# Two expert networks reordered: bias products one expert later, routing in pieces, the last expert's first layer early and its activation by blocks

## What is computed

```python
def _L1_ffn_ref(x, Wr, Wi, bi, Wo, bo):      # 8 experts, top 2
    router_logits = jnp.einsum('th,eh->te', xf, Wr)
    topk_vals, topk_idx = jax.lax.top_k(router_logits, TOP_K)
    routing_weights = jax.nn.softmax(topk_vals, axis=-1)
    h = jax.nn.gelu(jnp.einsum('th,efh->etf', xf, Wi) + bi[:, None, :], approximate=False)
    expert_out = jnp.einsum('etf,ehf->eth', h, Wo) + bo[:, None, :]
    ...
def expert_ffn(x, W1, B1, W3, B3, W2, B2):   # L2_ffn, 8 experts and a shared one
    g = swiglu((jnp.einsum('td,edh->teh', x, W1) + B1) * (jnp.einsum('td,edh->teh', x, W3) + B3))
    return jnp.einsum('tei,eid->ted', g, W2) + B2
def swiglu(h):
    xg = jnp.minimum(h[..., ::2], LIMIT)
    xl = jnp.clip(h[..., 1::2], -LIMIT, LIMIT)
    return xg * jax.nn.sigmoid(ALPHA * xg) * (xl + 1.0)
```

## Time and profile before

| | |
|---|---|
| median of 3 runs | 1476.81 us (1475.11, 1476.81, 1479.4) |
| profiled execution, its own time | 1474.77 us |
| its span | 1472.9 us |
| mean granted clock of PE | 0.967 of 2.4 GHz |
| first expert network | about 786 to 903 us of the span |
| second expert network | about 991 to 1307 us |

### The profile page before, as it was taken

How to read it: one execution, slowest core, us unless ns; L and a number is a source line. 1 busy time by engine, 2 the same in 40 slices (tenths; PEclk the granted TensorE clock), 3 DMA queues, 4 the chain that set the end, 5 groups by cost and what they waited for, 6 DMA issues and landing times.

```text
span 1472.9 us, 24074 instructions
## 1 busy us (share of the span) xinstructions
PE 1365.5 (93%) x10014; PEld 1159.6 (79%) x10014; DVE 986.2 (67%) x1782; ACT 773.5 (53%) x1246; POOL 207.3 (14%) x103
## 2 busy tenths in 40 slices
PE   9999999999999798888798999788999999987998
PEld 8999433899433795687697999777999999976976
DVE  8746777646777657566677677676577677757455
ACT  3446888435888354354544454544355544435433
POOL 0110876000876000102001000000000000000100
PEclk9999999999999999999899999899999999988999
DMA  8456353246363131035243453163454555041100
GB/s 346 118 197 210 92 178 86 71 159 211 100 175 91 65 130 54 0 141 208 81 171 130 149 168 125 28 231 129 133 190 167 193 189 193 34 195 74 54 1 22
DMA packets 30834, 194.81 MB, mean 132 GB/s; under 512 B 4211, under 2 KB 4339, under 8 KB 14726
## 3 DMA queue, kind: packets, MB, share of 16 engines
q1 hardware_dynamic: 30726, 193.27, 38.6%
HBM read 183.03 MB, written 3.93 MB: 127 GB/s over the span
## 4 chain that ended last, share of the span: by engine, by line
PE 75%; DVE 13%; ACT 6%; POOL 3%; issue 1%; DMA 0%; DVEq 0%; SPq 0%; ACTq 0%; POOLq 0%
PE PS L357 59%; PE PS L977 6%; PE PS L986 5%; PE PS L362 3%; DVE WL L300 2%; POOL WK L1172 2%; PE PS L618 1%; PE PS L459 1%; POOL WL L307 1%; DVE SM L534 1%; ACT WH L293 1%; DVE SM L1344 1%; ACT WK L1729 1%; DVE WK L1754 1%; DVE WK L1759 1%
## 5 line engine op out<-in xcount | busy, mean ns | idle before, releaser
L300 DVE TENSOR_TENSOR WL<-w,WH 128x768 fp32r<-128x768 f32 x373 | 355.0, 963 | 211.6 <-ACT WH L293 208.9
L293 ACT ACTIVATE WH<-w 128x768 fp32r<-128x768 f32 x381 | 315.9, 841 | 271.9 <-PE PS L357 258.1
L357 PE MATMUL PS<-XS,WH 128*128 128x256 f32 x2292 | 417.9, 285 | 11.4 <-DVE XS L484 7.1
L357 PEld LDWEIGHTS PS<-XS,WH 128*128 128x128 f32 x2292 | 355.8, 190 | 15.6 <-issue 12.0
L357 PE MATMUL PS<-XS,WL 128*128 128x256 f32 x1146 | 324.0, 283 | 0.0
L357 PEld LDWEIGHTS PS<-XS,WL 128*128 128x128 f32 x1146 | 217.6, 190 | 0.0
L1110 DVE TENSOR_TENSOR WK<-PS,WK 128x1024 f32<-128x1024 f32 x128 | 156.7, 1224 | 55.5 <-ACT PS L1054 54.5
L1172 POOL TENSOR_TENSOR WK<-WK 128x1024 f32<-128x1024 f32 x64 | 152.8, 2390 | 206.0 <-ACT WK L1051 206.0
L357 PE MATMUL PS<-WH,GS 128*128 128x256 f32 x864 | 162.0, 286 | 8.0 <-DVE GS L484 6.5
L1054 ACT ACTIVATE PS<-PS 128x1024 f32<-128x1024 f32 x128 | 129.4, 1011 | 34.4 <-PE PS L977 34.4
L357 PEld LDWEIGHTS PS<-WH,GS 128*128 128x128 f32 x864 | 137.1, 192 | 10.6 <-DVE GS L484 7.4
(11 more groups left out here) (252 smaller groups left out, 2014.3 us busy)
## 6 DMA issues: line engine op xcount, KB each, us to landing
w<-f2W_in SPq DMA_DIRECT2D x40, 1152.0 KB, 5.5
w<-Wrel_in SPq DMA_DIRECT2D x12, 1152.0 KB, 7.8
WK<-qrep_in SPq DMA_DIRECT2D x16, 768.0 KB, 5.5
w<-f1Wi_in SPq DMA_DIRECT2D x8, 1152.0 KB, 6.6
w<-f1Wo_in SPq DMA_DIRECT2D x8, 1152.0 KB, 5.1
w<-f3Wqkv_in SPq DMA_DIRECT2D x6, 1152.0 KB, 13.5
RT<-qg_rows SPq DMA_DIRECT2D x16, 384.0 KB, 6.3
RT<-AS SPq DMA_DIRECT2D x32, 192.0 KB, 6.7
```

The lines of the kernel that those rows point to most:

```text
L293: A.e.activation(w_hi(i), w_raw(i), ACT.Copy).then_inc(*hi("w", i))
L300: V.e.tensor_tensor(w_lo(i), w_raw(i), w_hi(i), ALU.subtract).then_inc(*lo("w", i))
L357: ins = T.e.matmul(o, l, r, start=i == 0 and first, stop=i == n - 1 and last, skip_group_check=lint)
```

## The change

All in the two expert networks; no matmul is added or removed.

- First network, PE: up(0), first tile of up(1), logits, rest of up(1), down(0), transpose of the routing weights (`comb_pe`), up(2), bias products, down(1), and on as before. DVE does the routing in three pieces, ahead of the second and third block of expert 1 and behind the third, copies to XN at the head of expert 2, and adds the bias after expert 2's blocks. ACT's Exp stands after expert 1's blocks.
- Second network, first experts: the routing comes in six pieces, one after each block of b(0); PE's order is a(0), logits, b(0), a(1), transpose, down(0), bias products, b(1).
- Second network, every expert up to 7: the clamp of hl now waits for the clamp of hg (`gated`).
- Second network, last expert: PE's order is a(7), down(6), b(7), a(8), b(8), down(7), down(8), with the weights fetched in that order. Its activation is done block by block: clamp of hg after block 2, then for each of blocks 3 to 5 the other three DVE instructions and ACT's upper part; ACT feeds one weight tile ahead of each upper part. The three lower parts follow after block 5.
- `vec_top2` is split into `top2_rank` (one row half) and `top2_pick`, `vec_softmax8` loses its first two instructions to `vec_less8`, with the same instructions in them.

```diff
-if e:
+if 0 < e < 8:
     main.append(("f2c" + str(e - 1), "f2W2", e - 1, 3, "V"))
 main.append(("f2b" + str(e), *(("f2W3", e) if e < 8 else ("f2Ws3", None)), 6, "V"))
+    main.append(("f2c7", "f2W2", 7, 3, "V"))
     main.append(("f2c8", "f2Ws2", None, 3, "V"))
...
-def bias_vec(name, n):
+def comb_vec(name, n):
     V.wait_ge(pe, name + "cT")
     V.e.tensor_copy(XN[0:n, 0:256], ps(name + "cT")[0:n, 0:256]).then_inc(*vec(name + "cT"))
+
+def bias_vec(name, down0):
     for m in range(2):
         for c0, c1 in ((0, 512), (512, 768)):
             V.wait_ge(pe, name + "b", m, c0)
+            V.wait_ge(vec, down0, 0, c0, m)
             V.e.tensor_tensor(x3[:, m, c0:c1], x3[:, m, c0:c1], ps(name + "b", m, c0)[:, 0:c1 - c0],
                               ALU.add).then_inc(*vec(name + "b", m, c0))
...
-    for e in range(8):
-        pe_gemm_T(("f1u", e), f1up(e), 0, 3, xs_at, lambda f: (act, "gelu", e, f),
-                  (lambda k: T.wait_ge(vec, "lower", "f1a", k - k % 2)) if e == 0 else None)
-        if e == 0:
-            logits_pe("f1z", "f1Wr", "f1a")
-        if e == 1:
-            bias_pe("f1", lg, 8, "f1bo")
-        if e:
-            down(e - 1)
+    def up(e, f0, f1, before=None):
+        pe_gemm_T(("f1u", e), f1up(e), f0, f1, xs_at, lambda f: (act, "gelu", e, f), before)
+
+    up(0, 0, 3, lambda k: T.wait_ge(vec, "lower", "f1a", k - k % 2))
+    up(1, 0, 1)
+    logits_pe("f1z", "f1Wr", "f1a")
+    up(1, 1, 3)
+    down(0)
+    comb_pe("f1", lg, 8)
+    up(2, 0, 3)
+    bias_pe("f1", 8, "f1bo")
+    down(1)
+    for e in range(3, 8):
+        up(e, 0, 3)
+        down(e - 1)
     down(7)
...
-        if e == 0:
+        if e == 1:
             act_softmax8("f1", lg)
...
+    def route(part_):
+        if part_ == 0:
+            V.wait_ge(pe, "f1z")
+            V.e.tensor_copy(lg, logits("f1z")).then_inc(*vec("f1zraw"))
+            top2_rank("f1", lg, 8, 0)
+        elif part_ == 1:
+            top2_rank("f1", lg, 8, 1)
+            top2_pick("f1", 8)
+            vec_less8("f1", lg)
+        else:
+            V.wait_ge(act, "f1exp")
+            V.e.tensor_tensor(lg, lg, sm2("f1sel", 8), ALU.mult).then_inc(*vec())
+            vec_norm8("f1", lg)
+            vec.also("f1comb")
+
     for e in range(8):
+        if e == 2:
+            comb_vec("f1", 8)
         for k in range(3):
             feed_vec(ahead(f1up(e) + k))
+            if e == 1 and k:
+                route(k - 1)
             vec_lower(GH[e % 2][:, 1, k, :], gtmp[:, k, :], GH[e % 2][:, 0, k, :], "gelu", e, k)
-        if e == 0:
-            V.wait_ge(pe, "f1z")
-            V.e.tensor_copy(lg, logits("f1z")).then_inc(*vec("f1zraw"))
-            sel = vec_top2("f1", lg, 8)
-            vec_softmax8("f1", lg)
-            V.e.tensor_tensor(lg, lg, sel, ALU.mult).then_inc(*vec())
-            vec_norm8("f1", lg)
-            vec.also("f1comb")
         if e == 1:
-            bias_vec("f1", 8)
+            route(2)
+        if e == 2:
+            bias_vec("f1", "f1d")
         if e:
             down(e - 1)
...
-        else:
+        elif e == 1:
+            comb_pe("f2", comb9, 9)
+            down(0)
+            bias_pe("f2", 9, "f2B2")
+        elif e < 8:
             down(e - 1)
         pe_gemm_T(("f2b", e), f2("b", e), 0, 6, xs_at, lambda f: (vec, "f2h3", e, f))
-        if e == 0:
-            bias_pe("f2", comb9, 9, "f2B2")
+    down(7)
...
+        elif e < 8:
             act_gemm_N(None, f2("c", e - 1), 3, 768)
-        act_gemm(f2("b", e), 6)
+        act_gemm(f2("b", e), 6 if e < 8 else 3)
         A.wait_ge(vec, "f2min", e)
         A.e.activation(sgb[i], hb[i][:, 0:3, :], ACT.Sigmoid, scale=1.702).then_inc(*act("f2sig", e))
-        A.wait_ge(vec, "f2g", e)
         if e >= 2:
             A.wait_ge(pe, ("f2d", e - 2), 512, 1)
-        act_upper(GH[i][:, 0, :, :], hb[i][:, 3:6, :], "f2g", e)
+        if e < 8:
+            A.wait_ge(vec, "f2g", e, 2)
+            act_upper(GH[i][:, 0, :, :], hb[i][:, 3:6, :], "f2g", e, 2)
+    for k in range(3):
+        feed_act(ahead(f2("b", 8) + 3 + k))
+        A.wait_ge(vec, "f2g", 8, k)
+        act_upper(GH[0][:, 0, k, :], hb[0][:, 3 + k, :], "f2g", 8, k)
+    act_gemm_N(None, f2("c", 7), 3, 768)
...
-    def route():
...
+    def route(f):
+        if f == 0:
+            V.wait_ge(act, "f2exp")
+            vec_norm8("f2", sc8)
+            V.e.tensor_tensor(sg, sc8, col("f2gb").unsqueeze(1).broadcast_to((P, 2, 8)), ALU.add).then_inc(*vec())
...
+        elif f == 4:
+            top2_rank("f2top", sg, 8, 0)
+        else:
...
     for e in range(9):
         i = e % 2
+        hg, hl = hb[i][:, 0:3, :], hb[i][:, 3:6, :]
         vec_gemm(f2("a", e), 6)
         if e == 0:
-            route()
-        else:
+            V.wait_ge(pe, "f2z")
+            V.e.tensor_copy(sc8, logits("f2z")).then_inc(*vec("f2zraw"))
+            vec_less8("f2", sc8)
+        elif e == 1:
+            comb_vec("f2", 9)
+            down(0)
+            bias_vec("f2", "f2d")
+        elif e < 8:
             down(e - 1)
 
...
+            if e == 0:
+                route(f)
+            if e == 8 and f == 2:
+                V.wait_ge(vec)
+                V.e.tensor_scalar(hg, hg, 7.0, None, ALU.min).then_inc(*vec("f2min", e))
+            if e == 8 and f >= 3:
+                gated(slice(f - 3, f - 2), f - 3)
+
+        def gated(ks, k):
+            V.wait_ge(vec)
+            V.e.tensor_scalar(hl[:, ks, :], hl[:, ks, :], 7.0, -7.0, ALU.min, ALU.max).then_inc(*vec())
+            V.wait_ge(vec)
+            V.e.scalar_tensor_tensor(out=hl[:, ks, :], in0=hl[:, ks, :], scalar=1.0, in1=hg[:, ks, :],
+                                     op0=ALU.add, op1=ALU.mult).then_inc(*vec())
+            V.wait_ge(vec)
+            V.wait_ge(act, "f2sig", e)
+            V.e.tensor_tensor(hl[:, ks, :], hl[:, ks, :], sgb[i][:, ks, :], ALU.mult).then_inc(*vec("f2g", e, k))
...
         vec_gemm(f2("b", e), 6, second)
-        hg, hl = hb[i][:, 0:3, :], hb[i][:, 3:6, :]
-        V.wait_ge(vec)
-        V.e.tensor_scalar(hg, hg, 7.0, None, ALU.min).then_inc(*vec("f2min", e))
-        V.e.tensor_scalar(hl, hl, 7.0, -7.0, ALU.min, ALU.max).then_inc(*vec())
-        V.wait_ge(vec)
-        V.e.scalar_tensor_tensor(out=hl, in0=hl, scalar=1.0, in1=hg, op0=ALU.add, op1=ALU.mult).then_inc(*vec())
-        V.wait_ge(vec)
-        V.wait_ge(act, "f2sig", e)
-        V.e.tensor_tensor(hl, hl, sgb[i], ALU.mult).then_inc(*vec("f2g", e))
-        vec_lower(GH[i][:, 1, :, :], hl, GH[i][:, 0, :, :], "f2g", e)
-        if e == 0:
-            bias_vec("f2", 9)
+        if e < 8:
+            V.wait_ge(vec)
+            V.e.tensor_scalar(hg, hg, 7.0, None, ALU.min).then_inc(*vec("f2min", e))
+            gated(slice(0, 3), 2)
+            vec_lower(GH[i][:, 1, :, :], hl, GH[i][:, 0, :, :], "f2g", e, 2)
+            for k in range(2):
+                vec.also("lower", "f2g", e, k)
+        else:
+            for k in range(3):
+                vec_lower(GH[0][:, 1, k, :], hl[:, k, :], GH[0][:, 0, k, :], "f2g", 8, k)
+    down(7)
```

More of the change, by code:

```diff
@@ L2188, in vec_top2, with vec_less8 @@
             return sel
-        def vec_softmax8(name, z):
+        def vec_top2(name, val, n):
+            for m in range(2):
+                top2_rank(name, val, n, m)
+            return top2_pick(name, n)
+        def vec_less8(name, z):
             mx = sm(name + "mx", 2)
@@ L2219, in bias_pe @@
             ins.then_inc(*pe(name + "cT"))
+        def bias_pe(name, n, width):
             T.wait_ge(vec, name + "cT")
@@ L2461, in down @@
                 pe_gemm_N(("f2d", e), f2("c", e), 3, 768, gh_at(e % 2), lambda c, m: (vec, "f2d", e, c, m),
-                          lambda k: T.wait_ge(vec, "lower", "f2g", e))
+                          lambda k: T.wait_ge(vec, "lower", "f2g", e, k))
             for e in range(9):
@@ L2483, in first @@
                     if e >= 2:
-                        A.wait_ge(vec, "lower", "f2g", e - 2)
+                        A.wait_ge(vec, "lower", "f2g", e - 2, 2)
                     b1 = col("f2Bs1", f, 1) if e == 8 else col("f2B1", e * 6 + f, 1)
@@ L2519, in down @@
                 vec_gemm_N(("f2d", e), f2("c", e), 3, 768, out_)
-            def route():
-                V.wait_ge(pe, "f2z")
-                V.e.tensor_copy(sc8, logits("f2z")).then_inc(*vec("f2zraw"))
-                vec_softmax8("f2", sc8)
-                vec_norm8("f2", sc8)
-                sg, gs = sm2("f2sg", 8), sm2("f2gs", 4)
-                V.e.tensor_tensor(sg, sc8, col("f2gb").unsqueeze(1).broadcast_to((P, 2, 8)), ALU.add).then_inc(*vec())
-                V.wait_ge(vec)
-                V.e.tensor_reduce(gs, sg.rearrange("p m (g a) -> p m g a", a=2), AX.X, ALU.add).then_inc(*vec())
-                keep = vec_top2("f2grp", gs, 4)
-                V.e.tensor_scalar(keep, keep, 1.0, -BIG, ALU.subtract, ALU.mult).then_inc(*vec())
-                V.wait_ge(vec)
-                for m in range(2):
```

(29 more changed lines are left out.)

38 lines of the change are left out of this document (22 added, 16 removed).

## The result

| | before | after |
| --- | --- | --- |
| median of 6 runs each, us | 1477.02 (1474.68 to 1485.66) | 1458.71 (1456.66 to 1467.35) |
| ratio after/before, 95% interval | | 0.9887 [0.9856, 0.9918] |
| profiled execution, its own time / span | 1474.77 / 1472.9 | 1458.04 / 1456.3 |

The change saves 18.3 us, 1.1%, beyond the 0.3% that counts here. The forecast was 1457.0 for the median and 1455.8 for the profiled execution.

What follows compares the result with a forecast made beforehand. TensorE, busy 93% of the span, bounds the kernel; only its waits and lower-clock time can be won. Gains of 24.3 less 5.3 of new waits net 19.0: 1455.8 profiled, 1457.0 with 1.2 added; range 1451 to 1463.

Steps and rivals of the forecast that it cites:

- First network, 6.4: First network: XN wait gone 3.2, bias products at full clock 1.5, dense matmuls no longer slowed 1.7; 6.4 us saved.
- 2.1 at expert 1: Second network, expert 1's first layer: routing pieces make VectorE's clamp late, so PE loses 2.1 us waiting for weights.
- 7 x 0.12: Second network, seven boundaries from expert 1 on: the added wait between two clamps costs 0.12 us each, 0.8 in all.
- 2.4 at the last expert: Last expert: split activation makes VectorE and ScalarE take turns, 3.8 us a block; waits of 0.75 and 1.65 us.
- The last expert's 7.2: End of second network: PE's 5.58 us wait goes, and 1.6 us of dense matmuls at the lower clock; 7.2 saved.
- Clock at the new waits: PE's waits of 2.1, 0.75 and 1.65 us may or may not bring the clock down; costed at nothing.
- The 1.5 us for the weight tile behind the unbroken routing: Second network's first expert: PE's wait for a weight tile goes, 1.5 us of the 10.7 saved there.
- no new wait: Rival for the whole change: VectorE fills its own gaps and all 24.3 us come; 1451.7 us, 12%.
- twice as long: Rival at the new waits: they are twice as long, 5.3 us more; 1462.3 us, 12%.
- the Exp comes so late: Rival in the first network: PE waits for the combine weights and the 6.4 us stay; 1463.4 us, 5%.
- slower: Rival at the second network's tight boundaries: wider ones keep bringing the clock down, 56 us lost; 1513 us, 2%.
- The clock falls at two of the new waits: Rival at the new waits: two clock falls at 1.7 us each, 3.4 us more; 1460.4 us, 18%.

Runs made afterwards that it cites:

- two-edit kernel: Kernel before with only the bias products one expert later in both networks and the last expert's first layers early; medians 1458.49 and 1457.55 us.
- the kernel with the cut router: Two-edit kernel with the router's 24 narrow passes cut into four between tiles of expert 0's first layer, in both networks; 1460.46 us.

## Why the prediction was right, point by point

The verdict and the place were right, and the sum was 2.2 us too low for the profiled execution (1455.8 against 1458.04). That the median came as close as 1.7 us is in part luck: the same kernel's other two series have 1465.83 and 1460.67, with clock falls in code that the change does not touch, and the first of them lies outside the stated range of 1451 to 1463.

- **First network, 6.4**: 6.24. It holds, and the runs without pieces show that the new place of the bias products alone makes it. No wait for the combine weights appeared.
- **Products at 2.7**: 2.84, from 5.48 at the lower level; they follow the clock.
- **2.1 at expert 1**: 2.19. The minimum starts at 1017.92, 2.7 us behind the layer's end on PE at 1015.2 (1000.78 + 6 x 2.15 + the fall's 1.5), where 2.5 was worked out. That the fall came ahead of it changed little: without it the wait was 2.25 and 2.34.
- **7 x 0.12**: 0.12 in the period; without the added wait 0.7 us of the stage came back.
- **2.4 at the last expert**: 0.84 + 1.40 = 2.24, block period 3.82 for 3.8. The cause is narrower than "DVE and ACT take turns": ACT rounds a weight tile one block too late.
- **The last expert's 7.2**: the 5.58 us wait and its fall are gone; by itself 7.2 in the stage and 7.3 in medians.
- **The 5.3 of new waits in all**: 310.70 against the 305.7 of the two-edit kernel at like clock, 5.0.
- **Clock at the new waits, costed at nothing**: nothing at 0.84 and 1.40 in any of the six profiles that have them. The 2.2 us wait saw a fall in two of seven, both times in the profiles without one behind the router's products. A fall costs 1.5 us, where 1.7 was taken. The Trainium skill, TensorE: Matmul & The Clock Gate, section "A second HAM failure mode: psum-queue depth-cycling", ties falls to short idle gaps between groups of matmuls; that was not borne out at 0.84 and 1.40 us, and at 2.2 us in two profiles of seven.
- **The step that was off** is "Clock at the new waits": it looked for falls only where PE pauses, and left the router's products out. The row it read a pause from, is itself such a group: 24 products of 128x2, near whose end the clock fell. It does so in all fourteen profiles, so pause and narrow products can't be told apart there. The fall behind the second network's router took 1.1 of the 1.9 us by which that network missed (10.7 for 12.6), by the 41.34 and 40.23 us above; the other 0.8 was not traced. The rest is 0.2 in the first network, and, where nothing was edited, 0.7 ahead of it, 0.2 behind the second, less 0.5 in the graph layer; together 2.4 us of span, 2.2 of the executions' own times.
- **The 1.5 us for the weight tile behind the unbroken routing** was no gain of its own: without the pieces the wait nearly goes too, and a clock fall stands in its place (26.52 for 26.29 us).
- **The rivals**: "no new wait" fell, all three chains are serial as said; "twice as long" fell, by 2.19, 0.84 and 1.40; "the Exp comes so late" fell, PE has no wait for XN; "slower" fell, no boundary from expert 1 on brought the clock down in any profile. "The clock falls at two of the new waits" fell as it was put, but one fall came in another place, and the median of 1458.71 lies midway between that rival's 1460.4 and the forecast.

Left open: what decides whether the clock falls, and whether the kernel before, with one profile, is free of the fall behind the router's products in every execution. A fall and a wait near it trade places (below), so the 5.3 us of new waits were worth less to remove than their length.

## What to carry to other kernels

Move the consumer of a late result a stage later before cutting the producer into pieces: here the move gave all of the first network's gain and the pieces gave none. Where two engines hand tiles to each other in turn, let the feeder run one tile ahead; one index took away 2.2 us of waits. Compare small parts by stages and single waits with the time at the lower clock beside them, because whole runs of one kernel differ by more than the part.

## What the runs showed that I had not expected

PE's clock falls without a pause. Of the twelve profiles of changed kernels with the router's products in one piece, ten show a fall of 3.4 us right behind those of the second network, though PE was busy throughout; the other two fell at the 2.2 us wait that followed. The one profile of the kernel before has none there. Behind the bias products of the second network all five profiles that lack the 2.2 us wait fell, and two of the other eight (one of the seven that have it, and the kernel with the cut router). In the first network a fall began behind the router's products, or in their last microsecond, in four of these twelve profiles, and the very same kernel has both (121.27 against 116.55 us). Both groups of products fill PE with few columns (128x8) or few rows (9x512); that this is the reason was not shown. Each fall had nearly the same size, 3.4 us at 1.2 GHz, or twice that, and cost 1.5 us per 3.4 where no wait behind it took the loss up.
